# Cross-attention scores in tiles of 64 stationary columns, and a new order of the steps on TensorE and around the last turn

## The reference

```python
x = x + self_attention(layernorm(x))      # causal, 32 query heads, 8 key heads of 16
x = x + cross_attention(layernorm(x), ctx)
x = x + ffn(layernorm(x))
# cross_attention, 32 query heads in 8 groups, 8 key and value heads of 128:
q = rmsnorm(hidden @ Wq.T) * q_w ;  k = rmsnorm(ctx @ Wk.T) * k_w ;  v = ctx @ Wv.T
scores = q @ k.T / sqrt(128) + mask          # each sequence against its own 64 keys
out = softmax(scores) @ v @ Wo.T
# ffn: relu(x up)^2 down + (x fc1 expert fc2) * (sum of the two largest gate logits), then a layernorm
```

## Time and profile before

| what | us |
|---|---|
| median of 3 runs | 1753.89 |
| lowest and highest | 1753.36, 1754.22 |
| the profiled execution's own time | 1748.64 |
| its span, first to last instruction | 1746.9 |
| PE busy | 1669.0 (96%) |
| DVE, ACT, POOL busy | 1065.2, 764.9, 654.9 |

### The profile page before, as it was taken

One profiled execution on the slowest core, in us unless ns is written; L12 is line 12 of the kernel. 1 busy time (PEld: TensorE's weight loads), 2 busy tenths in 40 slices (PEclk: granted clock), 3 DMA queues, 4 the chain that ended last, 5 costly groups with the idle time before them and its releaser, 6 DMA issues.

```text
span 1746.9 us, 32770 instructions
## 1 busy us (share of the span) xinstructions
PE 1669.0 (96%) x12760; PEld 1370.1 (78%) x12760; DVE 1065.2 (61%) x1977; ACT 764.9 (44%) x1396; POOL 654.9 (37%) x511
## 2 busy tenths in 40 slices
PE   5899899999999999899988999999999999998898
PEld 5566788888888888678875567888888888886797
DVE  4488666565665665764545876565656565657543
ACT  2575535354444453421226744445353544443221
POOL 3596423233233232550116944243233332335400
PEclk9999999999999999899999999999999999998999
DMA  4110011021010120211111102011010210201000
GB/s 168 60 43 1 21 42 61 0 60 42 18 60 18 42 66 0 73 49 38 59 60 51 31 1 60 3 60 31 29 60 0 60 44 16 66 25 61 7 19 25
DMA packets 26099, 71.14 MB, mean 41 GB/s; under 512 B 3120, under 2 KB 3376, under 8 KB 26032
## 3 DMA queue, kind: packets, MB, share of 16 engines
q1 hardware_dynamic: 26032, 70.22, 12.9%
HBM read 66.01 MB, written 4.19 MB: 40 GB/s over the span
## 4 chain that ended last, share of the span: by engine, by line
PE 85%; DVE 8%; POOL 3%; ACT 2%; issue 2%; DMA 1%; POOLq 0%; SPq 0%; DVEq 0%; ACTq 0%
PE acc L407 14%; PE acc L408 13%; PE acc L409 13%; PE y L407 9%; PE y L409 9%; PE y L408 9%; PE quad L665 7%; PE quad L692 4%; PE y L676 2%; PE quad L588 2%; DVE w_lo L1181 1%; POOL prob L1660 1%; PE quad L448 1%; PE acc L425 1%; DVE xn_lo L1181 1%
## 5 line engine op out<-in xcount | busy, mean ns | idle before, releaser
L1651 POOL TENSOR_TENSOR qkrs<-qkve,mhalf 128x10 f32<-128x10 f32 x64 | 124.9, 1952 | 350.6 <-DVE qkve L1332 350.6
L1660 POOL TENSOR_TENSOR prob<-prob,pmax 128x512 f32<-128x512 f32 x128 | 133.9, 1046 | 288.1 <-DVE pmax L1240 287.7
L407 PE MATMUL acc<-w_hi,xn_hi 128*128 128x512 f32 (+1 forms) x576 | 229.0, 398 | 11.1 <-DVE xn_lo L1181 11.1
L407 PE MATMUL y<-w_hi 128*128 128x512 f32 x576 | 232.7, 404 | 1.9 <-issue 1.9
L1326 DVE TENSOR_REDUCE qkss<-kbd 128x4 f32<-128x512 f32 x128 | 87.8, 686 | 234.5 <-ACT kbd L879 234.5
L408 PE MATMUL y<-w_lo,w_hi 128*128 128x512 f32 x576 | 226.0, 392 | 0.0
L409 PE MATMUL y<-w_hi,w_lo 128*128 128x512 f32 x576 | 226.0, 392 | 0.0
L408 PE MATMUL acc<-w_lo,xn_hi 128*128 128x512 f32 (+1 forms) x576 | 222.4, 386 | 0.0
L409 PE MATMUL acc<-w_hi,xn_lo 128*128 128x512 f32 (+1 forms) x576 | 220.6, 383 | 0.0
L1647 POOL TENSOR_TENSOR w_lo<-stage,w_hi 128x1024 fp32r<-128x1024 f32 (+1 forms) x88 | 169.9, 1939 | 111.6 <-ACT w_hi L845 111.6
L1666 POOL TENSOR_TENSOR prob<-prob,prec 128x512 f32<-128x512 f32 x128 | 148.4, 1159 | 79.7 <-DVE prec L1248 79.7
(11 more groups left out here) (129 smaller groups left out, 3716.4 us busy)
## 6 DMA issues: line engine op xcount, KB each, us to landing
stage<-in_w_cross SPq DMA_DIRECT2D x64, 512.0 KB, 3.6
stage<-in_w_cross SPq DMA_DIRECT2D x32, 256.0 KB, 3.0
stage<-in_w_ffn SPq DMA_DIRECT2D x16, 512.0 KB, 3.4
x<-in_x SPq DMA_DIRECT2D x8, 512.0 KB, 3.7
stage<-in_w_self SPq DMA_DIRECT2D x8, 512.0 KB, 4.5
kt<-in_ctx SPq DMA_DIRECT2D x16, 256.0 KB, 2.9
out_x<-x SPq DMA_DIRECT2D x16, 256.0 KB, 2.0
stage<-in_w_self SPq DMA_DIRECT2D x4, 256.0 KB, 3.4
```

The costliest lines, as they stand in the source:

```text
L407: nc.tensor.matmul(target, l_hi, r_hi, start=first, stop=False)
L1651: return nc.gpsimd.tensor_tensor(target, source, mhalf[:, 0:width], ALU.pow)
L1660: nc.gpsimd.tensor_tensor(pr, pr, spread(pmax[:, buffer, :], 8, SEQ), ALU.subtract).then_inc(s_sub.sem, 1)
```

## The change

Three edits go together. (1) `scores2` issues two matmuls of 64 stationary columns where one had 128, one for each pair of heads, into the two halves of the partitions of its bank. (2) TensorE's loop body is cut at another place: the scores and the transposes that stood at the start of a pass stand at the end of the pass before. The scores and transposes of the first pass move ahead of the loop, those of the second chunk's scores among them. (3) The steps before the loop and of the last turn, on all four compute engines, stand in a new order, and in the table `FFN` the third layernorm tile comes after the first latent tiles.

```diff
-FFN = ("ln0 ln1 ln2 lat00 lat01 ln3 up00 ...
+FFN = ("ln0 ln1 lat00 lat01 ln2 ln3 up00 ...
@@ TensorE, self_attention, its end
                 project_out(at, NT - 1, NT)
+                scores2(first, 0)
                 project_chunk_kv(first, 2)
-                scores2(first, 0)
                 project_chunk_q(first, 2)
                 second_norm(7)
+                scores2(first, 1)
+                transpose_probs2(first.at, 0, -2)
-            def scores2(place, k):
+            def scores2(place, k, after=None):
-                pe.wait_ge(ot_lo_done.sem, at(ot_lo_done, max(k - 1, 0)))
+                pe.wait_ge(ot_lo_done.sem, at(ot_lo_done, max(k - 1, 0) if after is None else after))
...
-                            ins = nc.tensor.matmul(quad[:, i, t * SEQ:(t + 1) * SEQ],
-                                                   q2t[rows, t, j].rearrange("p h q -> p (h q)"),
-                                                   k2t[rows, t, j, first:first + SEQ], start=j == 0, stop=j == 3)
+                            for h in range(2):
+                                ins = nc.tensor.matmul(
+                                    quad[h * SEQ:(h + 1) * SEQ, i, t * SEQ:(t + 1) * SEQ],
+                                    q2t[rows, t, j, 2 * h:2 * h + 2, :].rearrange("p h q -> p (h q)"),
+                                    k2t[rows, t, j, first:first + SEQ], start=j == 0, stop=j == 3)
-            def transpose_probs2(at, k):
+            def transpose_probs2(at, k, tile):
-                pe.wait_ge(y_free.sem, at(y_free, max(2 * k - 1, -1)))
+                pe.wait_ge(y_free.sem, at(y_free, tile + 1))
@@ TensorE, slot
-                scores2(place, k + 1)
-                transpose_probs2(place.at, k)
                 project_chunk_kv(place, k + 3)
                 values2(place, k, k + 2)
                 project_chunk_q(place, k + 3)
                 outputs(place, k, 0)
                 outputs(place, k, 1)
+                scores2(place, k + 2)
+                transpose_probs2(place.at, k + 1, 2 * k)
@@ TensorE, last_turn_and_ffn
-                scores2(turn, 1)
-                transpose_probs2(turn.at, 0)
                 project_chunk_kv(turn, 3)
                 values2(turn, 0, 2)
                 project_chunk_q(turn, 3)
+                transpose_probs2(turn.at, 1, -2)
+                scores2(turn, 2)
+                pe.wait_ge(pt_done.sem, turn.at(pt_done, 2))
                 outputs(turn, 0, 0)
-                scores2(turn, 2)
-                transpose_probs2(turn.at, 1)
+                values2(turn, 1, 3)
                 outputs(turn, 0, 1)
-                values2(turn, 1, 3)
+                transpose_probs2(turn.at, 2, 0)
                 norm(0)
+                pe.wait_ge(pt_done.sem, turn.at(pt_done, 3))
                 outputs(turn, 1, 0)
+                values2(turn, 2, 3)
+                norm(1)
                 outputs(turn, 1, 1)
-                scores2(turn, 3)
-                transpose_probs2(turn.at, 2)
-                norm(1)
-                values2(turn, 2, 4)
-                norm(2)
+                scores2(turn, 3, after=3)
                 latent(0)
                 outputs(turn, 2, 0)
+                norm(2)
+                outputs(turn, 2, 1)
+                transpose_probs2(turn.at, 3, 4)
                 norm(3)
-                outputs(turn, 2, 1)
-                transpose_probs2(turn.at, 3)
                 up(0, 0)
                 values2(turn, 3, 4)
```

The other three engines follow the same order. Before the loop, ACT does `sibling_keys(0)` and `exps(0)` before the second queries of chunk 1 and before chunk 2, and DVE does `masked_scores(0)` and `row_max(0)` ahead of `scale_chunk(1)`. In the last turn the order on DVE becomes this (POOL and ACT likewise put the steps of the probabilities ahead of the splitting of the FFN's weights):

```diff
                 variance(turn.at, 3)
-                updated(0)
-                scale_chunk(turn.at, 3)
-                final_statistics(0)
                 masked_scores(turn.at, 2)
                 row_max(turn.at, 2, 2)
+                updated(0)
+                final_statistics(0)
+                sums(turn.at, 2, 2)
+                outputs_lo(turn.at, 1)
+                norm(0)
+                updated(1)
+                final_statistics(1)
+                scale_chunk(turn.at, 3)
+                norm(1)
                 transposed(turn, 3)
-                updated(1)
-                norm(0)
-                outputs_lo(turn.at, 1)
-                final_statistics(1)
-                sums(turn.at, 2, 2)
-                norm(1)
+                outputs_lo(turn.at, 2)
                 norm_lo(0)
+                norm_lo(1)
                 updated(2)
                 final_statistics(2)
-                updated(3)
-                norm(2)
                 masked_scores(turn.at, 3)
                 row_max(turn.at, 3, 3)
...
@@ GpSimd, last turn
+                subtract_max(turn.at, 2, 2)
+                layernorm_rstd(at, 0, 0)
+                normalise_probs(turn.at, 2, 2)
                 split_piece(place, 0)
-                layernorm_rstd(at, 0, 0)
-                subtract_max(turn.at, 2, 2)
+                layernorm_rstd(at, 0, 1)
                 split_piece(place, 1)
-                layernorm_rstd(at, 0, 1)
-                normalise_probs(turn.at, 2, 2)
                 split_piece(place, 2)
...
```

More of the change, by code:

```diff
@@ L55 @@
     ["lx5", "lx6", (1, C_KV), (1, C_Q), (1, C_Q + 1), (2, C_KV), (2, C_Q), (2, C_Q + 1), "lx7"])}
-FFN = ("ln0 ln1 ln2 lat00 lat01 ln3 up00 up01 latt0 ln4 ln5 lat10 lat11 up02 up03 ln6 ln7 latt1 "
+FFN = ("ln0 ln1 lat00 lat01 ln2 ln3 up00 up01 latt0 ln4 ln5 lat10 lat11 up02 up03 ln6 ln7 latt1 "
        "up10 up11 up12 up13 lat20 lat21 latt2 up20 up21 up22 up23 lat30 lat31")
@@ L1029, in self_attention @@
                 queries(first, 1, 0)
+                sibling_keys(first.at, 0)
                 queries(first, 1, 1)
-                sibling_keys(first.at, 0)
+                exps(first.at, 0, 0)
                 keys_and_values(first, 2)
@@ L1034, in self_attention @@
                 queries(first, 2, 0)
-                exps(first.at, 0, 0)
                 queries(first, 2, 1)
@@ L1114, in last_turn_and_ffn @@
                 slot(turn, 0, next_group=False)
+                evacuate_probs2(turn.at, 1)
+                exps(turn.at, 2, 2)
+                outputs_hi(turn.at, 1)
                 split_piece(place, 0)
+                evacuate_probs2(turn.at, 2)
+                norm_hi(0)
                 split_piece(place, 1)
-                evacuate_probs2(turn.at, 1)
+                outputs_hi(turn.at, 2)
+                norm_hi(1)
+                sibling_keys(turn.at, 3)
                 split_piece(place, 2)
-                exps(turn.at, 2, 2)
-                sibling_keys(turn.at, 3)
-                outputs_hi(turn.at, 1)
-                norm_hi(0)
+                exps(turn.at, 3, 3)
+                norm_hi(2)
                 split_piece(place, 3)
-                evacuate_probs2(turn.at, 2)
-                norm_hi(1)
-                outputs_hi(turn.at, 2)
-                norm_hi(2)
-                exps(turn.at, 3, 3)
+                evacuate_probs2(turn.at, 3)
+                norm_hi(3)
                 split_piece(place, 4)
-                norm_hi(3)
                 split_piece(place, 5)
-                evacuate_probs2(turn.at, 3)
                 rectify(0, 0)
@@ L1416, in self_attention @@
                 updated(7)
+                masked_scores(first.at, 0)
+                row_max(first.at, 0, 0)
                 scale_chunk(first.at, 1)
+                transposed(first, 1)
                 key_squares(first, 2)
-                masked_scores(first.at, 0)
-                transposed(first, 1)
-                row_max(first.at, 0, 0)
                 second_norm(7)
+                sums(first.at, 0, 0)
                 query_squares(first, 2, 0)
-                sums(first.at, 0, 0)
                 query_squares(first, 2, 1)
@@ L1540, in last_turn_and_ffn @@
                 variance(turn.at, 3)
-                updated(0)
-                scale_chunk(turn.at, 3)
-                final_statistics(0)
                 masked_scores(turn.at, 2)
                 row_max(turn.at, 2, 2)
-                transposed(turn, 3)
-                updated(1)
-                norm(0)
-                outputs_lo(turn.at, 1)
-                final_statistics(1)
-                sums(turn.at, 2, 2)
-                norm(1)
+                updated(0)
[7 more added lines that the diff above has]
+                norm(1)
+                transposed(turn, 3)
+                outputs_lo(turn.at, 2)
                 norm_lo(0)
+                norm_lo(1)
                 updated(2)
                 final_statistics(2)
-                updated(3)
-                norm(2)
                 masked_scores(turn.at, 3)
                 row_max(turn.at, 3, 3)
-                norm_lo(1)
+                latent(0)
+                norm(2)
+                updated(3)
                 final_statistics(3)
-                outputs_lo(turn.at, 2)
-                norm_lo(2)
-                latent(0)
                 sums(turn.at, 3, 3)
@@ L1567, in last_turn_and_ffn @@
                 updated(4)
-                norm_lo(3)
                 final_statistics(4)
```

(9 more changed lines are left out.)

3 lines of the change are left out of this document (removed).

## The result

The changed kernel takes 1770.58 us (median of 4 runs, 1768.73 to 1773.8) against 1753.62 us of before (4 runs): ratio 1.0104, 95% interval 1.0081 to 1.0127. The forecast was 1691.1 with a range of 1672 to 1742, so both the number and the direction were wrong. The profiled execution took 1769.46 us, its span is 1767.7 us, 20.8 more than before's.

A forecast was written before the change was run, and what follows sets the result against it. PE was taken to bound the kernel, busy in 96% of the span. Loops 46.5 - cut 1.4 + entry 1.7 + exits 16 = 62.8 us off 1748.64 gave 1685.8, plus 5.25 for the median: 1691.1, range 1672 to 1742.

The forecast's parts named there:

- issue, at some 0.007 us a pair, also stays under 0.058: Scores: eight loads started within 0.05 us, so issuing load and matmul pairs was claimed not to limit the 0.058 us round.
- The round of 0.058 us: Scores: eight tiles work together, each 64-column load setting a round of 0.058 us; 16 rounds for 128 pairs.
- the start and drain: Scores: 0.15 us plus 0.03 for the longer last round, added to 16 rounds of 0.058 to give 1.11 us.
- the term of 46.5 us: Both loops: scores fall from 1.94 to 1.11 us, saving 0.83 us in each of 2 x 28 chunks.
- Rival B: Scores: load and matmul take turns in a tile, 0.42 us saved a chunk instead of 0.83; 1715 us; chance 0.12.
- rival A: Loop jumps: instructions are fetched again at each jump because the body grows to 6.9 packets; 1713 to 1748 us; chance 0.25.
- I went through the new order with the lengths of the old rows: Exits: walking the reordered steps found only small new waits, 3 us left of 11, so 8 us gained a half.
- half clock would not follow these stalls: Exits: remaining stalls were held shorter than the old ones that half clock followed, so the clock was counted as kept.
- 16 us: Exits: gain of 8 us a half from the new order, the scores' own gain there included; bounds 10 and 20.
- The new cut by itself: Loop jumps: less covered by queued matmuls, priced at 0.1 us for each of 14 passes, 1.4 us lost.
- the entry's waits: Loop entry: the first values2's wait of 2.94 us was to grow to some 3.8; no wait seen for scores2(0).
- the entry's gain: Loop entry: quicker scores2(0), now ahead of project_chunk_kv(2), save 2 x 0.83 = 1.7 us.

## Why the prediction was wrong

It failed in three steps; each had its place in the text.

**Scores, the step "issue, at some 0.007 us a pair, also stays under 0.058".** The round of 0.058 us was right, and so was the start and drain: 1.09 us with half the pairs. The 0.007 was read from eight loads in 0.05 us; those stood in the queue behind a wait. It is the price of a pair that stands ready in a full queue, good for 32 pairs. Behind them a pair costs 11.4 ns on average, so the term of 46.5 us is 56 x 0.42 = 23.5. Rival B had the 1.52 us by luck: its mechanism, load and matmul in turn, is not what happens. The Trainium skill (TensorE: Matmul & The Clock Gate, Wait — 56ns, not 53.3ns?) has a floor of some 25 ns from matmul to matmul; the rows show 11.4 and 7 ns where tiles differ, so it does not hold between tiles.

**Instruction fetch, the step that gave rival A 0.25 and a price of 1.6 to 4.1 us a jump.** The counts were right: a body of 4.8 packets became 6.9. What was missing is that the number of blocks covered depends not only on the length but on where the body starts: 1753 instructions cover 7 blocks or 8, and only 7 stay. So A came true for one loop of two. It was also priced too low: two blocks in a row come late (3.3 and 0.8 us without a matmul on average), and the clock falls behind them, 6.6 us a jump, 39.5 in all. The Trainium skill (Runtime: NRT & Kernel Launch, Instruction fetch mechanics) has 128 KiB in blocks of 256 instructions. The table agrees: seven blocks and one fetched ahead would be the eight that it holds. That one is fetched ahead is inferred, not shown.

**Exit, the step "I went through the new order with the lengths of the old rows".** I counted the waits on `pt_done` and the order behind the scaling, and left out that `outputs_hi(k)` waits for TensorE's `outputs(k - 1, 1)`, since both use one buffer. In the old order `norm(0)` and `sibling_keys(3)` stood ahead of it. The new one put them behind it: 4.28 and 3.36 us of waits instead of 1.83 and 2.88, with half clock behind each. That half clock would not follow these stalls was the second error there. Of 16 us nothing came, and 3.7 were lost. These 3.7 are not the order's alone: 3.5 of them lie in the second exit, which has the wait of 2.42 us behind the scores that the first doesn't have. With 128 columns, where only the two waits are there, both exits take 58.00 us, 1.7 and 1.1 more than before; with quick scores and no third wait the exit takes 56.54. So the order turned 8 us of gain a half into none or a small loss, and the wait on issue behind the scores, most likely fetch in code without a jump, took the rest; the forecast had no term for it.

The new cut by itself was put at 1.4 us and costs nothing (0.41 us over the jump); the entry's waits came as said. Put together: forecast -62.8 us; scores +23.0, the fetch in the first loop +39.5 and the cut -1.4, exits +19.7, the entry's gain that did not show +1.5, and some 1.3 elsewhere, which is the +20.8 of the span.

The direction hung on the fetch in the loop alone: without it, with 34 instructions more at the start, the same change is 1.0% faster than before.

## What to carry to other kernels

Count the instructions of a hardware loop's body in the compiled program, and look for packets on the instruction queue while it runs. Near the limit, here between seven and eight blocks of 256, a few instructions anywhere ahead of it decide, and satisfied waits in an idle place can move it. Look at straight code too where hundreds of tiny matmuls follow each other: here a block lasted 1.5 us. A rate read from instructions that stood ready in a queue holds for as many as the queue has; for hundreds of tiny matmuls take it from a stretch that is longer. When steps are reordered, list for each what buffer it overwrites and who still reads that, and let nothing that the bottleneck needs soon stand behind it.

## What the runs showed of the hardware that was not expected

- Tiles of 32 rows and 64 columns, eight at a time, do a round of load and matmul in 0.058 us (the second round 0.106 behind the first), for the first 64 instructions.
- Behind those 64 a pair takes 11.4 ns on average (5.7 ns an instruction), in stretches of 8.3 and of 16.7 ns.
- A change between tiles of 64 and of 128 columns costs 0.16 to 0.19 us each time (one kernel, one chunk read).
- A jump back over up to seven blocks of 256 instructions costs no time on PE, even behind only four transposes (0.41 us from the transposes to the keys and values, no packet in the loop). Over eight, 5.5 us of queued matmuls are not enough cover if the next block is used up quickly (2.4 us of wait behind 17 pairs).
- Straight code can starve too: in seven of eight exits the last 1 to 29 of the 128 score matmuls, or the matmul behind them, came 1.3 to 2.4 us late.
